# Edge segments prepared one group sooner, the last tile's chain moved ahead of the feed-forward units, and edge pairs sorted by destination so that each column's matmuls cover a band of groups

## The chip, the cores and the metric

One Trainium2 chip, one of its cores (one program, core 0). The metric is the device time of one execution in microseconds; lower is better. A core has TensorE (PE, with its weight loads shown as PEld), VectorE (DVE), ScalarE (ACT), GpSimd (POOL) and the queue engine SyncE (SP). Every engine works through its own instructions in the order in which they were written and waits on semaphores.

## The reference

A deformable 3x3 convolution, a graph attention over tokens, and a mixture of four expert networks whose weights come from the attention. All is float32.

```python
# x: (4, 128, 32, 32); channel-normalised first
o = conv3x3(xn, offset_w) + offset_b              # 27 channels: 9 dy, 9 dx, 9 masks
sampled[k] = bilinear(xn, at base + (dy, dx)[k]) * sigmoid(mask[k])       # k = 0..8, 4 corners each
x = x + einsum(sampled, dcn_w)                     # 4096 tokens of 128 channels
h = (norm(x) @ W_gat).reshape(M, HEADS, NUM_EXPERTS)
src = concatenate([edge_index[0], loops]); dst = concatenate([edge_index[1], loops])
e = leaky_relu(a_src[src] + a_dst[dst], 0.2)
ee = exp(e - max over edges into dst)
alpha = ee / segment_sum(ee, dst)
agg = segment_sum(h[src] * alpha, dst)
scores = layernorm(agg).mean(heads); top 2 of 4 experts, softmax over the two
out = x + sum over experts of gate * (gelu(norm(x) @ W1[e] + b1[e]) @ W2[e] + b2[e])
```

There are 524,288 edges with random ends in 0..32767, and M = 4096 tokens. An edge whose destination is 4096 or more is dropped, and a source of 4095 or more is read as row 4095. So an edge with a destination below 4096 either has a source below 4095 (here called a pair; about 64 in each of the 128 partitions) or it counts for the last token, and those only need a histogram of destinations.

## The kernel before

**Set-up.** Four images (b = 0..3) come in, are transposed and normalised, written to DRAM as cells (a 2 KB cell holds four corners), and convolved for the offsets. `sampling(b)` (L1009) on VectorE turns an image's offsets into gather indices `idx_i` and corner weights; it ends with a copy that raises `sampled` (L1054). All four `sampling` calls come before the loop.

**The loop over 96 groups.** 32 tiles of 128 tokens, three groups of three taps each: m = 3t + g. GpSimd issues three indirect DMAs (L455) for a group, into one of two tile buffers, and waits for `turned` of the same group two tiles earlier. ScalarE scales seven of the twelve corners (L841), VectorE the other five in one instruction (`corners`, L1076). TensorE adds the corners while transposing (`turn`, L571, 12 instructions), ScalarE evicts (L849), TensorE multiplies by the taps (`weigh`, L582), and VectorE adds the residual once per tile (`residual`, L1082).

Within the same loop, six groups (j = m % 6) to an edge segment `it` of 256 edges per partition, 16 segments: `edge_keys` makes keys that put pairs first, `keep` is one round of MAX8 and MATCH_REPLACE8 (L1158, L1160; eight rounds find the largest 56), `unpack_kept`, two one-hot instructions `hot(0)`, `hot(1)` (L1174, bf16, 128x3584), 28 histogram matmuls on TensorE (`count_edges`, L600, in the groups j = 0 and 1 of the next segment) and `add_counts` (L1128). The largest 16 keys of each segment go to `pairs1`. SyncE loads the segments into a ring of four, the first after all `sampling` calls.

From group 36 on, a unit of the feed-forward network (tile of 512 tokens, expert e; 32 units in all) is spread over every three groups: `up` twice (L625), gelu on ScalarE (L855), `down` (L636, 16 instructions) and `outputs` on VectorE (L1118). Units 0 to 19 lie in the loop.

**Between the loop and the pairs.** VectorE picks the 104 largest of the 256 keys of `pairs1` in rounds of eight (`pick_pairs`, L1218, L1219), the first 24 at once. Then follow the last residual, the last normalisation, the projection of image 3 (`project`, L615) and `token_rows` (L1137), whose rows go to DRAM (L366, L367) before GpSimd may gather source rows (L473, 10 DMAs a step). In TensorE's order units 20 and 21 stand ahead of the last tokens' transposes (L607), and units 22 and 23 ahead of `project`; units 24 to 28 follow. `unpack(0, 56)` splits the picked keys into codes; keys left over beyond 56 are collected over four partitions (`rest`), picked again (12 rounds) and spread back as 24 more columns. Low digits of the destinations are written to DRAM and broadcast to all partitions (L377), so that `turned_digits` (L1338) can build a one-hot that gathers the destination's terms with matmuls (`dst_logits`, L711).

**The pair loop.** Eight steps of ten columns, one pair per partition and column. For a column VectorE builds `code_hot` (L1311, 256 wide) and `spread` (L1312: the values times a one-hot over 16 groups of 20 values, 320 wide), and TensorE adds them into two banks (`add_pairs`, L721: four matmul instructions of 320 columns). A ring of five buffers lies between them (`NR`). In step p the next step is prepared between the columns: `hots` (L1291), `turned_digits`, then `dst_logits(p + 1)` on TensorE behind half of the columns, three multiply-and-reduce steps on VectorE (L1328, L1331), the logits, an exponential on ScalarE (L894), `weighted` (L1304). Units 29 to 31 are done in steps 0 to 3.

**The end.** Own and last-token terms (L1403 to L1412), the sums, layernorm, gates, and the gated sum of the experts (L1524), transposed and written out. If any capacity was exceeded (`lost`), a general path goes over all edges instead.

## Time and profile before

| | us |
|---|---|
| median of 3 runs | 779.71 (774.39 to 783.75) |
| the profiled execution | 772.18 |
| its span, first to last instruction | 770.4 |
| TensorE busy | 581.6 (75%) |
| VectorE busy | 549.9 (71%) |
| ScalarE busy | 363.0 (47%) |
| GpSimd busy | 411.8 (53%) |
| mean granted TensorE clock | 0.871 |
| bytes moved by DMA | 94.97 MB |

Busy shares are means over stages with different limits. A DMA issued by GpSimd occupies it for the duration shown, and another 0.30 us passes between two of them, which the profile calls "issue". "Remote" or "another core or an unknown queue" as a releaser means that the event that ended the wait was not matched to an instruction. The durations of vector instructions overlap the next one's start a little.

### The profile page before, as it was taken

The page shows a single profiled execution, that of the slowest core. Times are in us where ns is not written, and L with a number is a line of the kernel's source. Part 1 is how long each engine was busy: PE and PEld are TensorE (multiplying, and loading weights), DVE is VectorE, ACT ScalarE, POOL GpSimd, SP SyncE. Part 2 cuts the span into 40 slices and gives each one's busy share as a digit, 9 for nine tenths or more (in the row PEclk, how much of TensorE's full clock was granted, in tenths as well). Part 3 has the DMA queues.
Part 4 walks back from the last instruction along what each step waited for, and adds up shares of the span by engine and source line. Part 5 has one row for each costly group of instructions (what it writes and reads, how often), then busy time and mean ns, then how long its engine had stood idle before and what let it go on. Part 6 is the DMA issues. An engine that isn't in the chain of part 4 may idle for free.

```text
span 770.4 us, 11025 instructions
## 1 busy us (share of the span) xinstructions
PE 581.6 (75%) x3723; PEld 471.9 (61%) x3723; DVE 549.9 (71%) x1595; ACT 363.0 (47%) x1012; POOL 411.8 (53%) x401
## 2 busy tenths in 40 slices
PE   6772667756855987978978897998566799969716
PEld 4652667645754875867867695886354567646515
DVE  6825887658667583978658793794648677767897
ACT  5634456634834775856746774674312120000027
POOL 2071477667766766766876775700643455741023
PEclk9985789768878898989989997999978899979959
DMA  8661666556656666556666555600203611100002
GB/s 251 182 192 54 178 181 193 177 173 205 176 168 202 169 169 192 173 168 191 182 177 181 177 153 176 161 11 1 48 9 3 42 24 41 27 5 4 1 1 109
DMA packets 58197, 94.97 MB, mean 123 GB/s; under 512 B 21916, under 2 KB 36892, under 8 KB 58140
## 3 DMA queue, kind: packets, MB, share of 16 engines
q0 software_dynamic: 25600, 76.50, 35.1%
q1 hardware_dynamic: 32540, 17.75, 9.3%
q8 instruction: 30, 0.49, 0.3%
q14 instruction: 27, 0.22, 0.1%
HBM read 87.49 MB, written 6.71 MB: 122 GB/s over the span
## 4 chain that ended last, share of the span: by engine, by line
PE 55%; DVE 15%; issue 12%; ACT 10%; another core or an unknown queue 6%; DMA 1%; DVEq 0%; SPq 0%; ACTq 0%
PE bank L571 15%; PE bank L721 11%; PE bank L582 7%; PE bank L625 6%; ACT arena L841 5%; PE bank L636 5%; PE bank L600 4%; DVE x_tok L1524 2%; PE bank L550 2%; DVE scratch L1328 1%; PE bank L711 1%; DVE padded L1331 1%; ACT scratch L849 1%; ACT scratch L855 1%
## 5 line engine op out<-in xcount | busy, mean ns | idle before, releaser
L455 POOL DMA_INDIRECT arena<-cells,idx_i x288 | 314.1, 1090 | 179.8 <-issue 78.1
L841 ACT ACTIVATE arena<-arena,corner_w 128x128 f32<-128x128 f32 x672 | 206.5, 393 | 0.0
L571 PE MATMUL bank<-ident,arena 128*128 128x128 f32 x1152 | 168.3, 297 | 36.2 <-issue 21.2
L571 PEld LDWEIGHTS bank<-ident,arena 128*128 128x128 f32 x1152 | 146.3, 155 | 70.7 <-issue 58.2
L849 ACT COPY scratch<-bank 128x384 f32<-128x384 f32 x96 | 45.3, 472 | 164.2 <-remote 124.0
L473 POOL DMA_INDIRECT padded<-src_rows,pk_src x80 | 82.4, 1030 | 74.6 <-DVE act_gate L1345 48.1
L721 PE MATMUL bank<-scratch,arena 128*128 128x320 f32 x320 | 99.5, 465 | 23.0 <-DVE scratch L1312 21.8
L721 PEld LDWEIGHTS bank<-scratch,arena 128*128 128x128 f32 x320 | 63.6, 204 | 57.0 <-DVE scratch L1312 27.1
L582 PE MATMUL bank<-dcnw_sb,scratch 128*128 128x128 f32 x576 | 89.8, 292 | 10.9 <-issue 10.8
L582 PEld LDWEIGHTS bank<-dcnw_sb,scratch 128*128 128x128 f32 x576 | 79.4, 207 | 14.1 <-issue 14.1
L600 PE MATMUL bank<-padded 128*128 128x128 bf16 x448 | 44.2, 235 | 47.6 <-issue 47.4
L1076 DVE TENSOR_TENSOR arena<-arena,corner_w 128x640 f32<-128x640 f32 x96 | 78.8, 820 | 1.4
L636 PE MATMUL bank<-w_sb,scratch 128*128 128x128 f32 x512 | 66.1, 285 | 15.7 <-issue 13.9
L636 PEld LDWEIGHTS bank<-w_sb,scratch 128*128 128x128 f32 x512 | 63.4, 201 | 21.0 <-issue 18.5
L625 PE MATMUL bank<-chan,w_sb 128*128 128x512 f32 x128 | 70.8, 645 | 4.0 <-ACT scratch L855 2.7
L855 ACT ACTIVATE scratch<-bank,b_sb 128x512 f32<-128x512 f32 x64 | 44.0, 690 | 52.4 <-PE bank L625 21.9
L600 PEld LDWEIGHTS bank<-padded 128*128 128x128 bf16 x448 | 32.4, 105 | 56.0 <-issue 55.2
L1174 DVE TENSOR_TENSOR padded<-lanes,kept_lohi 128x3584 bf16<-128x3584 bf16 x32 | 64.6, 2019 | 0.3
L1082 DVE TENSOR_TENSOR x_tok<-bank,x_tok 128x128 f32<-128x128 f32 x32 | 9.2, 289 | 73.9 <-remote 47.3
L1158 DVE MAX8 kept<-keys 128x8 f32<-128x256 f32 x128 | 54.5, 426 | 3.2
L894 ACT ACTIVATE padded<-padded 128x40 f32<-128x40 f32 x8 | 1.9, 236 | 103.1 <-DVE padded L1300 88.2
L1160 DVE MATCH_REPLACE8 keys<-kept,keys 128x256 f32<-128x256 f32 x112 | 45.8, 408 | 0.0
(248 smaller groups left out, 661.9 us busy)
## 6 DMA issues: line engine op xcount, KB each, us to landing
arena<-cells,idx_i POOLq DMA_INDIRECT x288
scratch<-in_L_ffn_edge_index_dram SPq DMA_DIRECT2D x32, 128.0 KB
padded<-lo_rows SPq DMA_DIRECT2D x8, 320.0 KB
chan<-in_x_dram SPq DMA_DIRECT2D x4, 512.0 KB, 5.3
cells<-n_tok SPq DMA_DIRECT2D x4, 512.0 KB, 4.3
out_dram<-chan SPq DMA_DIRECT2D x8, 256.0 KB, 2.0
cells<-n_tok SPq DMA_DIRECT2D x4, 448.0 KB, 4.7
padded<-src_rows,pk_src POOLq DMA_INDIRECT x80
```

The source lines that it names most:

```text
L455: nc.gpsimd.indirect_dma_start(cell[:, u, k, :, :].rearrange("p c f -> p (c f)"), None, squares[t // TB], bass.IndirectOffsetOnAxis(ap=idx ...
L473: nc.gpsimd.indirect_dma_start(src_got[:, u, c, :], None, src_rows[:, :], bass.IndirectOffsetOnAxis(ap=pk_src[:, j:j + 1], axis=0)).then_i ...
L571: mm = nc.tensor.matmul(banks[m % 2][:, j * P:(j + 1) * P], cell[:, t % 2, 3 * g + j, c, :], ident[:, :], is_transpose=True, start=(c == 0 ...
L582: mm = nc.tensor.matmul(banks[2 + t % 2][:, 0:C], samp[:, t % 2, k, :], dcnw_sb[:, k, :], start=(k == 0), stop=(k == K - 1))
L600: mm = nc.tensor.matmul(hist, both[0], both[1], start=(c == 0), stop=(c == CAP // 2 - 1))
L625: nc.tensor.matmul(banks[4 + f][:, :], w1_sb[:, e, f * P:(f + 1) * P], chan[:, s * 512:(s + 1) * 512], start=True, stop=True).then_inc(up_ ...
L636: mm = nc.tensor.matmul(banks[6][:, q * C:(q + 1) * C], hid[:, (n % 2) * NF + f, q * P:(q + 1) * P], w2_sb[:, e, f, :], start=(f == 0), st ...
L721: mm = nc.tensor.matmul(sum_part[q], code_hot[:, r, q * P:(q + 1) * P], spread[:, r, :, :], start=False, stop=(last and col == SUB - 1))
L841: ins = nc.scalar.activation(cell[:, u, k, c, :], cell[:, u, k, c, :], ACT.Copy, scale=corner_w[:, t, k, c:c + 1])
L1076: V.tensor_tensor(spots, spots, weights.unsqueeze(2).to_broadcast([P, CORNERS - BY_ACT, C]), ALU.mult)\
L1158: done(V.max(top, ka))
L1174: ins = V.tensor_tensor(onehots[:, h, :, :].rearrange("p c (j f) -> p c j f", f=4), lanes[:, :, :].unsqueeze(1).to_broadcast([P, CAP, LO / ...
```

## The change

Twelve edits, in the order of the program:

- `sampling(2)` comes after the first segment's keys and rounds, `sampling(3)` after the first `corners`; the tiles of `sampling` lie in `arena`, and the edge loads no longer wait for it. `trow` is cleared before `sampling(0)`.
- In the loop the key rounds of segment it + 1 run in groups 3 to 5 of segment it, the one-hots in groups 1 and 2, the histogram matmuls in groups 3 and 4, `add_counts` in group 0 of the next segment.
- In the last segment's groups 3 to 5, where no next segment follows, the 56 own pairs are picked.
- Feed-forward units begin at group 33, so unit 20's `up` and `down(19)` also lie in the loop.
- The keys are turned (`turn_keys`), so that the picked pairs come sorted by destination, largest first.
- After the loop TensorE's order is `down(20)`, the digits' transpose, `up(21)`, the last tokens, `project`; units 22 to 24 follow, units 25 to 31 are done in the pair loop, one a step.
- `window(c)` gives each block of five columns a band of the 16 groups; `spread`, the matmuls on it, the one-hots and the destination terms cover the band only. A pair outside its band sets `lost`.
- The ring of `code_hot` and `spread` has 10 buffers for 5; source rows have three buffers for two; `lo_turned` has two for one.
- `dst_logits(p + 1)` comes first in TensorE's step p, and waits for `pair_lg` of the step before.
- The second and third digit broadcasts are issued earlier on SyncE.
- The own terms are worked out in steps 1 and 6 of the pair loop.
- Rounds are redistributed: 56 in the loop, 16 before `token_rows`, 32 after the first digits; the rest in 40 and 56.

```diff
-        NR = 5
+        NR = 10
...
-        PAIR_UNIT = 29
-        FIRST_UP = 36
-        HIST_SLOTS = {0: (0, 14), 1: (14, CAP // 2)}
+        PAIR_UNIT = 25
+        FIRST_UP = 33
+        HIST_SLOTS = {3: (0, 14), 4: (14, CAP // 2)}
+        BLOCK = 5
+
+        def window(c):
+
+            c0 = c // BLOCK * BLOCK
+            bounds = []
+            for k, z in ((c0 + BLOCK, 4.5), (c0 + 1, -4.5)):
+                rank = k * (1.0 - 1.0 / (9.0 * k) + z / (3.0 * k ** 0.5)) ** 3
+                bounds.append(min(max(int((1.0 - rank / 64.0) * GROUPS), 0), GROUPS - 1))
+            return bounds[0], bounds[1] + 1
...
-                        mm = nc.tensor.matmul(sum_part[q], code_hot[:, r, q * P:(q + 1) * P], spread[:, r, :, :],
-                                              start=False, stop=(last and col == SUB - 1))
+                        mm = nc.tensor.matmul(sum_part[q][:, lo * VAL:hi * VAL], code_hot[:, r, q * P:(q + 1) * P],
+                                              spread[:, r, 0:hi - lo, :], start=False, stop=(last and col == SUB - 1))
...
-            count_edges(NSEG - 1, 0, CAP // 2)
-            unit(n0)
-            unit(n0 + 1)
+            down(n0)
+            pe.wait_ge(pair_idx_ready, 1)
+            pe.wait_ge(conv_read, NT - 1)
+            early = OWN // SUB * SUB
+            nc.tensor.transpose(banks[2][0:early, 0:P], pk_lo_f[:, 0:early], ident[:, :]).then_inc(digits_turned, 1)
+            up(n0 + 1, 0)
+            up(n0 + 1, 1)
             pe.wait_ge(t_normed, B)
             turn_tokens(B - 1, 0, 0)
             pe.wait_ge(t_normed_a, 1)
             turn_tokens(B - 1, 1, 1)
-            unit(n0 + 2)
-            unit(n0 + 3)
-            pe.wait_ge(conv_read, NT - 1)
-            project(B - 1, 2)
+            pe.wait_ge(conv_read, NT)
+            project(B - 1, 3)
...
             for p in range(NSUB):
                 n = PAIR_UNIT + p
+                if p < NSUB - 1:
+                    dst_logits(p + 1)
+                if n < UNITS:
+                    up(n, 0)
+                    up(n, 1)
                 for e in range(NE):
-                    if e == NF and p < NSUB - 1:
-                        dst_logits(p + 1)
-                    if e < NF and n < UNITS:
-                        up(n, e)
-                    if e == NF and n <= UNITS:
-                        down(n - 1)
+                    if e == 3 and n < UNITS:
+                        down(n)
                     add_pairs(p, p % 2, e, last=(p == NSUB - 1))
...
+            sampling(0)
+            sampling(1)
+            edge_keys(0)
+            for rnd in range(CAP // 8):
+                keep(rnd)
+            sampling(2)
+            for m in range(3 * NT):
+                it, j = divmod(m, 6)
+                b = it // 4 - 1
+                corners(m)
+                if m == 0:
+                    sampling(3)
+                if j == 0:
+                    keep(CAP // 8)
+                    unpack_kept(it)
+                    if it >= 1:
+                        add_counts(it - 1)
+                if j == 1:
+                    done(V.tensor_copy(kept_lohi[:, :, :, :], kept_i[:, 1:3, :].unsqueeze(3).to_broadcast([P, 2, CAP, 4])))
+                    hot(0)
+                if j == 2:
+                    if it > 0:
+                        residual(2 * it - 1)
+                    hot(1)
...
+                if it + 1 < NSEG:
+                    if j == 3:
+                        edge_keys(it + 1)
+                        keep(0)
+                        keep(1)
...
+            for p in range(NSUB):
+                u = p % 2
+                spreads(p, u, 0)
+                if p < NSUB - 1:
+                    hots(p + 1, 1 - u)
+                    dst_sums(p + 1, 1 - u)
+                spreads(p, u, 1)
+                if p < NSUB - 1:
+                    logits(p + 1, 1 - u)
+                if PAIR_UNIT + p <= UNITS:
+                    outputs(PAIR_UNIT + p - 1)
+                spreads(p, u, 2)
+                if p < NSUB - 1:
+                    weighted(p + 1, 1 - u)
+                if p < NSUB - 2:
+                    turned_digits(p + 2)
+                spreads(p, u, 3)
```

## Rows read from the trace of the kernel before

**Rows 1.** Windows by stage: length; busy PE, PEld, DVE, ACT, POOL; clock, DMA share, GB/s.

```profile
78.00:294.00 216.00, 157.71 (x1158) 138.97 (x1159) 160.60 (x396) 127.35 (x397) 151.89 (x140) 0.82 0.63 183
294.00:511.00 217.00, 186.25 (x1397) 156.36 (x1397) 157.54 (x400) 139.51 (x408) 144.74 (x131) 0.91 0.58 167
511.00:588.00 77.00, 52.29 (x319) 40.44 (x317) 48.09 (x164) 25.58 (x40) 19.97 (x21) 0.90 0.08 15
588.00:730.00 142.00, 124.92 (x534) 88.81 (x534) 105.66 (x295) 13.54 (x20) 63.12 (x61) 0.92 0.20 20
```

**Rows 2.** The cell gathers of line 455: duration ns, and what ended their idle time.

```profile
L455 POOL DMA_INDIRECT arena<-cells,idx_i x288: 942/949/2725, 38.1 to 498.4; - x144
...
  remote: 35.2, 20
  PE bank L571: 33.9, 11
```

**Rows 3.** Timeline near 183 to 195 us: start, us, engine, line, operation [idle before].

```profile
184.70 0.27 PE L600 MATMUL bank<-padded 128*128 128x128 bf16 x2 [1.09 <-issue]
...
194.76 0.48 ACT L849 COPY scratch<-bank 128x384 f32<-128x384 f32 x1 [11.80 <-remote]
195.00 0.95 POOL L455 DMA_INDIRECT arena<-cells,idx_i  x1 [1.86 <-remote]
```

**Rows 4.** Timeline of VectorE: first corners of segments 4, 5, 8 and 9.

```profile
176.44 0.82 DVE L1076 TENSOR_TENSOR arena<-arena,corner_w 128x640 f32<-128x640 f32 x1
...
203.96 0.82 DVE L1076 TENSOR_TENSOR arena<-arena,corner_w 128x640 f32<-128x640 f32 x1
...
287.57 0.82 DVE L1076 TENSOR_TENSOR arena<-arena,corner_w 128x640 f32<-128x640 f32 x1
...
321.01 0.82 DVE L1076 TENSOR_TENSOR arena<-arena,corner_w 128x640 f32<-128x640 f32 x1
```

**Rows 5.** Timeline of the loop's start.

```profile
71.62 0.15 DVE L1054 COPY act_gate<-ident 128x1 f32<-128x1 f32 x1
...
78.02 0.76 DVE L1076 TENSOR_TENSOR arena<-arena,corner_w 128x640 f32<-128x640 f32 x1
...
81.99 0.95 POOL L455 DMA_INDIRECT arena<-cells,idx_i  x1 [21.26 <-PE bank L571]
```

**Rows 6.** Timeline from the last corners to the first values of the pairs.

```profile
510.79 0.82 DVE L1076 TENSOR_TENSOR arena<-arena,corner_w 128x640 f32<-128x640 f32 x1
...
515.61 0.43 DVE L1218 MAX8 pairs<-pairs 128x8 f32<-128x256 f32 x1
...
516.60 0.43 DVE L1218 MAX8 pairs<-pairs 128x8 f32<-128x256 f32 x1
...
533.29 1.88 PE L625 MATMUL bank<-chan,w_sb 128*128 128x512 f32 x4
...
535.01 1.95 PE L636 MATMUL bank<-w_sb,scratch 128*128 128x128 f32 x16
...
536.80 1.86 PE L615 MATMUL bank<-wgat_sb,chan 128*128 128x24 f32 x16
...
558.17 3.75 PE L636 MATMUL bank<-w_sb,scratch 128*128 128x128 f32 x16 [6.97 <-issue]
...
587.72 0.15 DVE L1345 COPY act_gate<-ident 128x1 f32<-128x1 f32 x1
```

**Rows 7.** Groups by shape in the pair loop (588 to 731 us): busy us, mean ns, idle.

```profile
L721 PE MATMUL bank<-scratch,arena 128*128 128x320 f32 x320 | 99.5, 465 | 23.0 <-DVE scratch L1312 21.8 <-issue 1.0
...
L1312 DVE TENSOR_TENSOR scratch<-scratch 128x320 f32<-128x320 f32 x80 | 38.7, 484 | 0.0
...
L711 PE MATMUL bank<-a_dst_heads,chan 128*128 128x128 f32 x140 | 16.9, 276 | 0.1
...
L1328 DVE TENSOR_TENSOR scratch<-bank,scratch 128x512 f32<-128x512 f32 x14 | 9.7, 692 | 24.3 <-PE bank L711 13.5 <-remote 7.6 <-issue 3.1
...
L1291 DVE TENSOR_TENSOR scratch<-iota_f,pk_group 128x160 f32<-128x160 f32 x7 | 2.2, 318 | 0.0
...
L1328 DVE TENSOR_TENSOR scratch<-bank,scratch 128x256 f32<-128x256 f32 x7 | 3.0, 424 | 0.2
```

**Rows 8.** The chain of waits, its last stretch of line 721: start, us, what.

```profile
715.37 14.28 PE bank L721 x52
```

453 lines of the change are left out of this document (239 added, 214 removed).

## The prediction

> **What bounds the kernel now.** I read the windows by stage first, then who held up GpSimd's gathers, then timelines where stages meet, then the groups of the pair loop by shape. Four stretches matter.
>
> *The loop, 78 to 511 us.* No compute engine is full: TensorE 73% and 86%, VectorE 74% and 73% of the two halves [rows 1]. GpSimd is: it shows 151.89 us for 140 gathers, and each has 0.30 us behind it, so 151.9 + 42 = 194 of 216 us, and 144.7 + 39 = 184 of 217 [rows 1]. The fastest gather takes 0.94 us, so a group of three can't take less than 3.75 us; 90 groups are 338 us of the 417 from 82.0 to 499. Of the other 79, some 39 us are gathers that take up to 2.7 us instead of 0.95 (296.6 us for 271 of them), and the rest are waits: 35.2 us "remote" and 33.9 us for line 571, of which 21.3 us is the one before the loop, so 48 us with the 0.30 us that each wait swallows [rows 2, 5]. A wait of GpSimd follows a slow stretch of TensorE like the one in rows 3: for some 10 us each pair of instructions starts 0.7 us after the last though it waits for nothing that the profile names, and ScalarE does not see the turned group for 11.80 us. GpSimd loses only 1.9 us, since it is up to six groups ahead. I count one such stretch in nearly every segment.
>
> *Loop to pairs, 511 to 588 us.* VectorE is busy 48.1 of 77 us and TensorE 52.3 [rows 1], and neither runs through: the last corners are at 510.79, the projection ends at 536.80 + 1.86 = 538.7, the first values of the pairs are there at 587.72 [rows 6]. TensorE loses 6.97 us at 558 in front of unit 26's `down`, and as much once more at 571 [rows 6].
>
> *The pair loop, 588 to 730 us.* Line 721 takes 277 ns an instruction at full clock (14.28 / 52 = 0.275) [rows 8] and has 320 of them. TensorE's work at full clock is 320 x 0.2775 = 88.8 us of columns, 140 instructions of line 711 at about 0.12 = 16.8, three pairs of ups at 1.88 and four downs at 1.95 [rows 6] = 13.4: 119 us. Actual: 142. TensorE is first, VectorE (105.7 us) not far behind, and 23 us go in handing over: TensorE waits 21.8 us for `spread`, VectorE 24.3 us for line 711 [rows 7], and part of the stretch runs at the lower clock, 0.92 in the mean [rows 1].
>
> *The end*, 770.4 - 729.7 = 40.7 us, is not touched.
>
> **The change, part by part.**
>
> *Start of the loop.* `sampling(2)` ends at 71.62, corners start at 78.02 because `sampling(3)` and the clearing of `trow` lie between [rows 5]. The first corners can follow at 71.7, so the first group is turned 6.3 us sooner and GpSimd resumes at 75.7 instead of 81.99. The second corners now wait for `sampling(3)` (78.0), the last round and the unpacking, about 79.2, against 82.2 before, and GpSimd waits some 3 us for them. From the fourth group on it is about 4.8 us ahead; I take -4.8 (ends: -3, -6.3). The first segment's keys and rounds (8 us) fall where VectorE waited 11 us for TensorE's offsets. If that cover were gone, they would delay `sampling(2)` by 8 us. The edge loads go onto SyncE's queue behind the cells' writes, with nothing behind them for a long time.
>
> *Inside the loop.* The same instructions are issued; only their groups change. VectorE's work of a segment stays some 20 us in 27, so GpSimd remains the bound and the long gathers stay. New waits: `add_counts` in group 0 waits for matmuls of two groups before (formerly of three groups before), and behind it in VectorE's order stands the next corners. `hot_ready` is already implied by the corners that TensorE waits for. A slow stretch of TensorE then holds VectorE one group's work more, about 3 us, which GpSimd's lead of six groups (22 us) still covers, as it covers 11.8 us now [rows 3]. One more unit goes in (4 us of TensorE, off the path). I take 0 for the loop. Ends: all 48 us of GpSimd's waits vanish, but one wait a segment belongs to TensorE's stretches, so a gain of 25; or every segment loses 1 us, 15.
>
> The skill has a view on those stretches. The Trainium skill, "Runtime: NRT & Kernel Launch", section on instruction fetch mechanics, says that instructions come in 16 KiB blocks of 256, fetched ahead, and that crossing a block is mostly hidden. If that were all, a TensorE that waits for nothing would not slow down, and the trace disagrees: 11.80 us behind one stretch. By it the loop would fall to GpSimd's 375 us and the total by up to 48 us more. What causes the stretches no row tells; I let them stay.
>
> *Loop to pairs.* VectorE's 48 us lose: seven rounds at 0.99 us [rows 6], moved into the last segment, -6.9; five `outputs` at 0.69, -3.4; the own logits, about -1.9; `hot(1)` and the hit mask, -3; half of the destination reductions, -1.7; one more `turned_digits` +0.9 and the bound checks +1: 33 us. Its idle 29 us shrink, because TensorE's order loses units 22 and 23 ahead of `project` (two times 1.75 + 1.75 = 7.0 us between starts [rows 6]) and the histogram, and because fewer of VectorE's steps wait for a unit: the two stretches of 7 us hit `outputs` before, and now only units 21 to 23 are consumed here. What stays late: the rows' way to DRAM and back, the digits' broadcast, and the rest's way over four partitions. They are DMA round trips, three times some 4 to 7 us, and only partly under rounds. I take 21 of the 29 us: 33 + 21 = 54 instead of 77, -23. Ends: idle 13 (46) and 29 (62). Two SyncE broadcasts moved forward stand in front of the rest's spreading, but wait on `turned_digits`, which is done by then.
>
> *Pair loop, TensorE.* The formula gives bands of 6, 8, 10, 12, 13, 14, 14, 13, 12, 11, 10, 9, 9, 8, 7 and 6 groups of 20 values for the sixteen blocks of five columns: 162 of 256, 63%. A 24-column instruction takes 1.86 / 16 = 0.116 us [rows 6]; that is the floor. Above it I scale 0.2775 by columns / 320 (0.104 for six groups, hence 0.116; 0.243 for fourteen). The sixteen blocks sum to 2.83 us, times 20 instructions: 56.6 us instead of 88.8, -32. Line 711 is already near the floor (0.12 at 128 columns), so its narrowing gives nothing. Units 25 to 31 cost 7 x (1.88 + 1.95) = 26.8 instead of 13.4. Total 56.6 + 16.8 + 26.8 = 100 us instead of 119.
>
> *Pair loop, VectorE.* From 484 ns at 320 and 318 at 160 elements, an element costs 1.04 ns [rows 7]; 202 on average instead of 320 saves 0.12 us a column, 9.8 in all. The reductions (692 at 512, 424 at 256: 1.05 ns) narrow by 30%: -5.6; the one-hots -1. Four more `outputs` +2.8, own logits +1.9. So 105.7 - 16.4 + 4.7 = 94 us. The two engines are nearly even, 100 and 94, and taken step by step the larger of the two (TensorE in steps 2 and 3 with 16 us, VectorE in the first two and step 6 with 13 to 15) sums to 108.
>
> *Handing over.* The ring of 10 and the early `dst_logits` remove what made TensorE wait 21.8 us, yet nearly even engines wait for one another more, and at step 2 and 3 VectorE must wait for TensorE's last three columns. Of the 23 us that 142 has above 119 I let 9 stay above 108: 117, so -25. Ends: 108 (nothing left) and 128 (the same 19% on top). The third buffer of source rows lets GpSimd run further ahead, off the path.
>
> **Sum.** 770.4 - 4.8 + 0 - 23 - 25 = 717.6 us of span, about 719 for the profiled execution (before: 772.2). The median of the runs lies 7.5 us above the profiled execution. With the same distance: 727 us.
>
> **Rivals.**
> - *The hand-over keeps the gain* (0.2). Shorter matmuls only make TensorE wait for VectorE, whose 94 us plus the waits for line 711 become the bound: pair loop 128 (+11); and the two 7 us stretches stay on the path ahead of it (+8), with one more in the denser pair loop (+4). 750 us. For it: both engines are near 100 us. Against: the ring is twice as deep.
> - *The loop gains too* (0.12). The histogram moved behind the groups that need it lets GpSimd's waits shrink by 25 to 30 us: 700 us. For it: 48 us of such waits. Against: the stretches are not caused by VectorE.
> - *The loop gets slower* (0.05), the other side. Segment 4 takes 27.5 us, segment 8 takes 33.4, and there the slow stretch fell on turns and weighs and VectorE waited for a conv result, and not on the histogram [rows 4]. If moving the histogram puts the stretch on the turns in every segment, each of 15 costs 5.9 us more: +88, 815 us. It decides from 53 / 15 = 3.5 us a segment.
> - *The change doesn't do what it says* (0.01). One pair outside its band starts the general path, thousands of gathers at 1.25 us: milliseconds. The bands are cut at 4.5 deviations, so I give it almost nothing.
>
> **How the numbers follow.** The forecast has 0.62, with its own ends 712 (unprofiled, pair loop 108, idle 13) and 742. The range takes in the first rival and part of the second: 706 to 754. Faster by over 1% (about what can be told from no change) holds for the first three cases: 0.94; slower takes the last two, 0.05; within 1%: 0.01.
>
> **What would show it.** Right: the first gather after the pause near 76 us; the last corners near 506; the projection's end 18 to 19 us after them and not 28; the pair loop's start some 54 us after them; line 721 in shapes from 120 to 280 columns with 57 to 65 us at full clock; the pair loop at 110 to 125 us; the last 41 us as before. Wrong: segments of 30 us and more, which means the loop; TensorE idle behind `spread` for over 20 us in the pair loop; or gaps of 7 us called "issue" between the projection and the pairs.

## The result, and the profile after

The kernel after takes 770.55 us in the median of 20 runs, the kernel before 777.9 us on the same chip; the ratio is 0.9875, with a 95% interval of 0.984 to 0.991. Ratios, here and below, leave out executions more than 1.5% longer than the fastest of the same kernel, while the medians include them. So it is 1.2% faster, where the forecast said 727 us, 6.5% faster, and 706 to 754. The profiled execution took 774.0 us and its span is 772.3.

The stages, cut at events that every kernel has (all from the timelines; "band matmuls" are those of `add_pairs`, L721 before and L753 after; the forecast's column is its own sum):

| us from the span's start | before | forecast | after |
|---|---|---|---|
| first corners | 78.0 | about 71.7 | 74.7 |
| GpSimd resumes | 82.0 | 75.7 | 78.7 |
| last corners | 510.8 | 506 | 514.2 |
| first values of the pairs | 587.7 | 560 | 595.1 |
| first band matmul | 588.6 | 561 | 601.1 |
| last band matmul ends | 729.6 | 677 | 731.5 |
| span | 770.4 | 717.6 | 772.3 |

Against the forecast the last corners come 8 us late, the way to the pairs' first values takes 81 us instead of 54 (+27), the pair loop 136.4 instead of 117 (+19), and the end is as forecast. In spans the miss is 54.7 us and in medians 43.5, because the 7.5 us that the forecast added from three runs of the kernel before did not come again: here the median lies 3.5 us below the profiled execution. Before's lines for the same stretches are in [rows 1]. After, by windows (an engine's busy us and instructions, then granted clock, DMA share, GB/s):

```profile
core 0: us, PE busy (x) PEld busy (x) DVE busy (x) ACT busy (x) POOL busy (x), PEclk, DMA share, GB/s
...
514.00:595.00 81.00, 43.57 (x246) 35.67 (x245) 37.12 (x143) 17.25 (x33) 29.57 (x31) 0.73 0.10 19
595.00:731.50 136.50, 109.99 (x600) 93.44 (x599) 92.83 (x312) 28.94 (x36) 49.37 (x51) 0.87 0.19 18
731.50:772.30 40.80, 14.76 (x97) 12.89 (x96) 33.32 (x97) 21.80 (x62) 10.72 (x16) 0.75 0.14 52
```

Work did go. VectorE does 37.1 us between the loop and the pairs (48.1 before; the forecast left it 33, so 4 us of what it took off stayed) and 92.8 in the pair loop (105.7; forecast 94). TensorE's band matmuls lost what was forecast, 31.5 us of busy time against 32 (all forms, 320 instructions, busy us and mean ns; before 99.5 and 465 in the same view):

```profile
L753 PE MATMUL bank<-scratch,arena 128*128 128x120 f32 (+8 forms) x320 | 68.0, 363 | 26.2 <-DVE scratch L1286 14.1 <-issue 12.1
```

Yet the time stayed. The largest piece of the chain of waits says where, 25.4 us in one piece, and the waits name three engines at the same moment:

```profile
558.64 25.40 another core or an unknown queue
```

```profile
584.11 1.26 ACT L895 ACTIVATE scratch<-bank,b_sb 128x512 f32<-128x512 f32 x2 [37.21 <-remote]
584.13 0.69 DVE L1152 TENSOR_TENSOR arena<-bank,b_sb 128x512 f32<-128x512 f32 x1 [25.49 <-remote]
...
585.42 1.43 PE L665 MATMUL bank<-w_sb,scratch 128*128 128x128 f32 x5 [25.09 <-ACT scratch L895]
```

VectorE stood for 25.5 us in front of an `outputs` (L1152) whose matmuls (L665) had ended at 558.3; ScalarE stood in front of matmuls (L654) that had ended at 560.3, and TensorE behind ScalarE. Only one engine worked, GpSimd. The windows over that stretch:

```profile
550.00:558.00 8.00, 7.72 (x36) 7.75 (x37) 4.70 (x17) 0.00 (x0) 6.06 (x7) 0.50 0.25 54
558.00:566.00 8.00, 2.34 (x6) 0.81 (x5) 0.61 (x3) 0.00 (x0) 5.98 (x7) 0.93 0.10 9
566.00:575.00 9.00, 0.00 (x0) 0.00 (x0) 0.00 (x0) 0.00 (x0) 6.87 (x8) 0.50 0.11 11
575.00:584.00 9.00, 0.00 (x0) 0.00 (x0) 0.00 (x0) 0.00 (x0) 3.19 (x4) 0.50 0.05 5
```

GpSimd issues the gathers of the pairs' source rows, and these move little: 10% of the DMA engines, some 10 GB/s. Nothing else was under way: the digits' broadcast that SyncE had issued at 552.85 shows in the 54 GB/s of 550 to 558 us and no longer in the 9 to 11 GB/s behind it. With the third buffer it issued 30 in one unbroken row (0.30 us between two of them), where before it issued 20 (544.0 to 569.3) and then waited for `pair_used`:

```profile
541.10 1.19 POOL L501 DMA_INDIRECT padded<-src_rows,pk_src  x1 [3.85 <-DMA dst_rows<-a_dst]
542.58 0.94 POOL L501 DMA_INDIRECT padded<-src_rows,pk_src  x1 [0.30 <-issue]
...
578.17 0.94 POOL L501 DMA_INDIRECT padded<-src_rows,pk_src  x1 [0.30 <-issue]
...
595.56 1.00 POOL L501 DMA_INDIRECT padded<-src_rows,pk_src  x1 [16.45 <-DVE act_gate L1330]
```

VectorE's last instruction ends at 558.7 us and TensorE's at 560.3, 18 to 19 us and 14 to 15 gathers after the row began, and they resume at 584.1, 5 us after its last gather ended. A second row of 20, from 595.6 to 620.9, has a slow stretch at 607 to 624 us. This one sets in 11 us and 9 gathers after its row began, and from 609.6 us on a broadcast of SyncE is under way in it (DMA share 0.85 in 607 to 616 us, at 9 GB/s). In the trace of before the row of 20 ends at 569.3, and the VectorE step that the prediction's "second stretch of 7 us" hit starts at 569.8. The edge loop has rows of up to 18 gathers, and the slow stretch of [rows 3] lies at the end of one of them (below).

### The profile page after: what moved, and what is told of

It is laid out like the page before. It is cut to its first block, busy times and chain, and to the rows that moved or that the text cites. A ratio compares the mean times of both kernels' runs of the same rounds, so it can differ in the third digit from the quotient of the medians.

```text
span 772.3 us, 11071 instructions
## 1 busy us (share of the span) xinstructions
PE 563.0 (73%) x3723; PEld 475.0 (62%) x3723; DVE 534.5 (69%) x1609; ACT 370.6 (48%) x1018; POOL 407.7 (53%) x433
## 4 chain that ended last, share of the span: by engine, by line
PE 49%; DVE 18%; issue 12%; another core or an unknown queue 10%; ACT 9%; DMA 2%; SPq 0%; DVEq 0%; ACTq 0%
PE bank L598 13%; PE bank L609 6%; PE bank L753 6%; PE bank L654 6%; ACT arena L881 5%; PE bank L665 5%; PE bank L578 4%; PE bank L629 3%; DVE x_tok L1604 2%; PE bank L742 2%; DVE arena L1110 1%; DVE padded L1209 1%; PE bank L644 1%; ACT scratch L889 1%
## 5 line engine op out<-in xcount | busy, mean ns | idle before, releaser
L598 PE MATMUL bank<-ident,arena 128*128 128x128 f32 x1152 | 166.4, 294 | 39.4 <-issue 22.4
L598 PEld LDWEIGHTS bank<-ident,arena 128*128 128x128 f32 x1152 | 144.6, 153 | 77.3 <-issue 62.4
L889 ACT COPY scratch<-bank 128x384 f32<-128x384 f32 x96 | 45.3, 472 | 166.0 <-remote 125.3
L501 POOL DMA_INDIRECT padded<-src_rows,pk_src x80 | 78.2, 978 | 72.0 <-DVE act_gate L1330 45.3
L609 PE MATMUL bank<-dcnw_sb,scratch 128*128 128x128 f32 x576 | 91.5, 293 | 14.6 <-issue 13.2
L753 PE MATMUL bank<-scratch,arena 128*128 128x120 f32 (+8 forms) x320 | 68.0, 363 | 26.2 <-DVE scratch L1286 14.1
L665 PE MATMUL bank<-w_sb,scratch 128*128 128x128 f32 x512 | 66.8, 286 | 25.5 <-ACT scratch L895 25.3
L665 PEld LDWEIGHTS bank<-w_sb,scratch 128*128 128x128 f32 x512 | 64.0, 202 | 27.5 <-ACT scratch L895 26.2
L753 PEld LDWEIGHTS bank<-scratch,arena 128*128 128x128 f32 x320 | 56.6, 204 | 37.8 <-issue 16.7
L654 PE MATMUL bank<-chan,w_sb 128*128 128x512 f32 x128 | 73.3, 667 | 3.6 <-issue 3.6
L629 PE MATMUL bank<-padded 128*128 128x128 bf16 x448 | 41.3, 237 | 35.2 <-issue 34.9
L1116 DVE TENSOR_TENSOR x_tok<-bank,x_tok 128x128 f32<-128x128 f32 x32 | 9.3, 289 | 71.2 <-remote 52.8
L1152 DVE TENSOR_TENSOR arena<-bank,b_sb 128x512 f32<-128x512 f32 x24 | 16.5, 686 | 29.1 <-remote 25.5
```

The lines of the kernel that those rows point to most:

```text
L501: nc.gpsimd.indirect_dma_start(src_got[:, u, c, :], None, src_rows[:, :], bass.IndirectOffsetOnAxis(ap=pk_src[:, j:j + 1], axis=0)).then_i ...
L598: mm = nc.tensor.matmul(banks[m % 2][:, j * P:(j + 1) * P], cell[:, t % 2, 3 * g + j, c, :], ident[:, :], is_transpose=True, start=(c == 0 ...
L609: mm = nc.tensor.matmul(banks[2 + t % 2][:, 0:C], samp[:, t % 2, k, :], dcnw_sb[:, k, :], start=(k == 0), stop=(k == K - 1))
L629: mm = nc.tensor.matmul(hist, both[0], both[1], start=(c == 0), stop=(c == CAP // 2 - 1))
L654: nc.tensor.matmul(banks[4 + f][:, :], w1_sb[:, e, f * P:(f + 1) * P], chan[:, s * 512:(s + 1) * 512], start=True, stop=True).then_inc(up_ ...
L665: mm = nc.tensor.matmul(banks[6][:, q * C:(q + 1) * C], hid[:, (n % 2) * NF + f, q * P:(q + 1) * P], w2_sb[:, e, f, :], start=(f == 0), st ...
```

## The experiments

**Theory A:** a long unbroken row of GpSimd's indirect gathers makes the other engines' issue and the events between them late, from some 16 to 18 us after its start until GpSimd pauses; the third buffer made the row longer and so gave back what the rest of the change gained. **Theory B:** the stretches are TensorE's own (its instruction supply), and the missing time has other causes: the third buffer's traffic, the denser pair loop, VectorE as the bound. Each group of runs had its own runs of the kernel before on its chip: 770.45 us in the median for the first four, 771.21 for the next four, 777.91 for the four after those, 775.21 for the last three. A ratio is to those.

**One step less of lead in the pair loop** (the kernel after; a lead of two steps, three buffers)

```
-                if p >= GOT:
-                    pool.wait_ge(pair_used, p - GOT + 1)
+                if p >= 2:
+                    pool.wait_ge(pair_used, p - 1)
```

> The changed kernel with GpSimd allowed two pair steps ahead instead of three (the third source buffer stays). Theory A (an uninterrupted run of GpSimd's gathers holds back TensorE's issue and its semaphores until GpSimd pauses): GpSimd stops after 20 gathers, at about 566 us, so the stretch that began near 558 and ended at 584.1 ends near 570; the pairs start some 12 to 14 us sooner and the time is 755 to 760 us, ratio to the kernel before 0.97 to 0.975. Rival B (the stretch has nothing to do with the third buffer, but with what TensorE or the digit broadcasts do): the stretch stays about 25 us long, time 768 to 773, ratio 0.985 to 0.99.

738.78 us, ratio 0.958 [0.954, 0.962]: a larger gain than either theory expected. The first row of gathers is 20 long again (526.7 to 552.0), and the `outputs` behind it waits 10.75 us, until 555.26, instead of 25.49. From the last corners to the first band matmul it is 71.2 us instead of 86.9. One wait in GpSimd's order is worth 3% of the kernel.

The profiled executions are 34 us apart, and 14 of these lie ahead of the edit: the last corners come at 500.4 us instead of 514.2. That stretch has the same instructions in both. In the other variants whose order is untouched up to there (full width; paced pairs twice, and at full width; the iotas between pair steps) they come between 504.6 and 511.2 us. So the place of a stage in a single execution can be off by 5 to 10 us, and the profiled execution of the kernel after is the slowest of these there.

**The third buffer alone, in the kernel before** (`src_got` with three buffers, GpSimd up to three steps ahead)

> The kernel before with three buffers of source rows instead of two, nothing else. Theory A: GpSimd's run in front of the pairs grows from 20 to 30 gathers (544 to about 581 us), the wait of 5.75 us that VectorE had at 569.8 grows by up to 12 us, time +8 to +12 us, ratio 1.01 to 1.015. Rival B: the same time, ratio 1.0 within 0.3%, or slightly faster since GpSimd is further ahead.

780.46 us (768.8 to 783.6; 4 runs) beside 770.45 (758.1 to 779.8): +10 us in the median, but the runs overlap and no interval is on record. Its first row is 30 long (548.5 to 586.2) and from the last corners to the first band matmul it takes 92.6 us instead of 77.8. Part of the 15 us comes back in its pair loop, 129.3 instead of 141.0 us. The stages bear out theory A, the longer row and the later pairs; that this part of the change is a loss in time by itself is likely and not shown.

**Windows of the full width** (the kernel after)

```
-            return bounds[0], bounds[1] + 1
+            return 0, GROUPS
```

> The changed kernel with every band set to all 16 groups, so each column's matmuls have 320 columns again and VectorE builds 320 elements. If the sum of the prediction holds, TensorE's work in the pair loop rises from 100 to 132 us at full clock and the time by 20 to 32 us, to 790 to 802, ratio 1.015 to 1.03. Rival: the pair loop is bound by handing over and by slow stretches and not by the columns, so the narrowing is worth 10 us or less: 771 to 781, ratio 0.99 to 1.004.

768.02 us in the median, ratio 1.004 [0.998, 1.010]. Against the kernel after nothing is lost by the medians, but these were taken beside runs of before that differ by 7 us (770.45 and 777.9). The ratios, each to its own runs of before, lie 1.6% apart (0.9875 there) and their intervals do not meet: some 12 us, between the two expectations. The band matmuls take 89.4 us instead of 68.0, and from the first to the last of them it is 137.6 us instead of 130.4. The row of 30 is there, and the 25.0 us wait too.

**Four groups of lead in the edge loop instead of six** (the kernel after)

```
-                        pool.wait_ge(turned, 3 * (t - 2) + g + 1)
+                        pool.wait_ge(turned, 3 * (t - 2) + g + 3)
```

> The changed kernel with the cell gathers of the loop held to four groups ahead of the turned group instead of six (waits for two more groups to be turned). Theory A: the slow stretches of TensorE last until GpSimd pauses; with a shorter lead GpSimd pauses sooner, so they shrink from some 10 us to 3 us and the waits of ScalarE (11.8 us) with them; the loop keeps its length or gets up to 20 us shorter: 750 to 771 us. Rival B: the stretches have a length of their own (10 us); a lead of four groups (15 us) less the landing no longer covers them, and the loop grows by 3 to 6 us a stretch, 16 of them: 815 to 865 us.

755.71 us, ratio 0.976 [0.971, 0.982]. ScalarE's "remote" waits for the turned groups fall from 125.3 us (the longest 11.8) to 65.2 (4.9). The row of 30 and its 25.0 us wait stay. In the profiled executions the edge loop takes 432.6 us instead of 439.5 and the stretch of the band matmuls 124.8 instead of 130.4.

**Pairs paced** (the kernel after, the lead of three steps kept; GpSimd waits between two steps until the ten gathers of the earlier one have landed)

```
                 if p >= GOT:
                     pool.wait_ge(pair_used, p - GOT + 1)
+                if p >= 1:
+                    pool.wait_ge(pair_in[(p - 1) % 3], 16 * SUB * ((p - 1) // 3 + 1))
```

> The kernel after, with GpSimd held in the pair loop until the ten gathers of its previous step have landed; its lead of three steps stays. Theory A (a run of more than some 14 gathers without a pause of GpSimd makes the other engines' issue and their semaphores late until it pauses; the kernel after starts 30 in a row at the loop's end): the run of 30 falls apart into three of ten, so the 25 us remote waits near 559 to 584 us go or shrink below 8 us, the pairs start some 60 us after the last corners instead of 81, the pair loop has no stretch of 1.0 to 1.7 us issue pieces, and the time is 725 to 742 us, as with a lead of two steps (738.8) or below it. Theory B (the lead of three steps itself costs, by the DMA traffic of the rows or by their buffers): the lead is the same as in the kernel after, so 765 to 775 us.

726.23 us, ratio 0.932 [0.925, 0.939]; 44 us less than the kernel after in the medians, 43 by the ratios, and that by one wait. The rows of ten have pauses of 3.4, 1.7 and 2.1 us between them (536.3 to 549.2, 552.6 to 564.8, 566.5 to 578.7, 580.8 to 594.0):

```profile
548.27 0.94 POOL L503 DMA_INDIRECT padded<-src_rows,pk_src  x1 [0.30 <-issue]
552.61 0.94 POOL L503 DMA_INDIRECT padded<-src_rows,pk_src  x1 [3.40 <-DMA padded<-src_rows,pk_src]
...
566.47 0.97 POOL L503 DMA_INDIRECT padded<-src_rows,pk_src  x1 [1.69 <-DMA padded<-src_rows,pk_src]
```

Its stages, from the last corners on:

```profile
509.60:571.90 62.30, 48.68 (x267) 39.15 (x266) 40.60 (x153) 18.17 (x32) 24.16 (x26) 0.78 0.14 29
571.90:693.00 121.10, 105.13 (x577) 89.07 (x575) 90.09 (x301) 28.15 (x35) 56.98 (x57) 0.92 0.22 17
693.00:734.00 41.00, 14.54 (x96) 12.71 (x96) 33.50 (x97) 21.80 (x62) 10.38 (x16) 0.75 0.14 52
```

62.3 us to the first band matmul instead of 86.9, with the same instructions, and no standstill on that way; then 121.1 instead of 130.4. In the pair loop a slow stretch stayed, in a row of ten that began at 580.8, behind a pause of 2.1 us:

```profile
584.00:597.00 13.00, 8.23 (x33) 6.86 (x33) 2.06 (x8) 0.00 (x0) 7.88 (x8) 0.63 1.10 14
```

```profile
596.64 0.66 DVE L1313 TENSOR_TENSOR arena<-bank,scratch 128x480 f32<-128x480 f32 x1 [10.94 <-remote]
```

VectorE waited 10.9 us there, and the DMA share was 1.10 while 14 GB/s moved, with a broadcast of SyncE under way. So the pauses removed the standstill of 25 us and not every slow stretch. Theory B about the lead falls: lead and buffers are those of the kernel after. So does B about the instruction supply for the standstill, since TensorE's and VectorE's programs are unchanged.

**The edge loop paced as well** (at every fourth group GpSimd waits for the landing of the group before)

```
+                    m = 3 * t + g
+                    if m >= 4 and m % 4 == 0:
+                        tp, gp = divmod(m - 1, 3)
+                        pool.wait_ge(cells_in[3 * (tp % 2) + gp], 48 * (tp // 2 + 1))
```

> The kernel after with the pairs paced as in the run before, and in the loop too: at every fourth group GpSimd waits until the gathers of the group before it have landed, so no run is longer than 12 gathers. Theory A: TensorE's slow stretches in the segments (0.7 us between pairs of instructions for some 10 us) vanish, the waits of line 571 and of the turns' groups with them; each pause costs some 2 us of GpSimd, 24 of them 48 us, against 47.5 us of GpSimd's waits that the loop has now, so the loop (424 us) comes out between 385 and 425 us and the whole at 690 to 740 us. Theory B (the stretches come from TensorE's own instruction supply): the stretches stay, the pauses are added, and the loop grows by 20 to 48 us over the run with paced pairs.

762.72 us, ratio 0.990 [0.985, 0.995], 36 us slower than with paced pairs alone. The late events mostly went, and GpSimd's own pauses cost more than they gave:

```profile
POOL arena L487 <- DMA arena<-cells,idx_i: 77.2, 21, 5.8
...
ACT scratch L895 <- remote: 55.7, 17, 8.6
...
DVE x_tok L1122 <- remote: 15.0, 6, 5.3
```

Line 895 is here what line 889 is in the kernel after. There ScalarE's waits were 125.3 us and VectorE's 52.8. But 77.2 us of pauses replace 41.0 us of GpSimd's "remote" waits, and from the first to the last corners it is 476 us instead of 438. The first corners came at 65.6 us instead of 71.7: the row of 18 gathers ahead of the loop is cut too.

**Both paced, windows of the full width**

> As the run before (both paced), but with windows of the full width. It asks what the narrow bands are worth once no stretch lies over the pair loop. The prediction's reasoning (columns bind TensorE in the pair loop: 32 us of columns less) makes it 15 to 30 us slower than the run before; the reasoning that VectorE and the hand-over bind makes it slower by 0 to 8 us, as full width was worth nothing measurable with the long runs in place.

776.94 us, ratio 0.997 [0.990, 1.004]: 14 us slower than the run before by the medians, 0.7% by the ratios. The stretch of the band matmuls is 136.7 us instead of 113.2 in the profiled executions; but this one's was the longest of its ten runs (788 us), so the two stretches can't be set side by side; the intervals of the two ratios overlap.

**The kernel before with both pacings**

> The kernel before with both pacings (its two buffers of source rows kept). Theory A: it gains too, since its loop has runs of 18 gathers and its pairs runs of 20: the two stretches of TensorE near 558 and 571 us shrink to one or none (-7), the stretch at 660 to 677 us goes (-5 to -10), the loop changes as it does in the run with both paced. So 730 to 765 us. The distance to the kernel after with both paced is then the change's own worth without the run of 30, and the prediction said 43 to 50 us. Theory B: 770 to 800 us, as only the pauses are added.

780.03 us, ratio 1.005 [0.999, 1.011]. It missed. Its pair loop has 129.7 us instead of 141.0, but the way to it stays (76.5 us), and its edge loop grew to 463.7 from 432.8.

**The kernel before with paced pairs alone**

> The kernel before, with only the pair loop's gathers paced to runs of ten (its two buffers of source rows kept, its other loop untouched). Before has a first run of 20. Both pacings cost its edge loop some 30 us and left its pair loop at 129.7 us of line 721 instead of 141, and the way from the last corners to it at 76.5 instead of 77.8. If the runs of 20 cost before only inside its pair loop: 758 to 764 us. The distance from there to the kernel after with paced pairs (726.2) is the change's own worth, 32 to 38 us. If pacing is worth as much to before as to after (44 us), it would come to 727 to 735 us, and the change would be worth nothing; if nothing, 771.

769.23 us, ratio 0.987 [0.982, 0.991] (0.9866 of 777.9), by the ratio in the expected place. So pacing is worth 1.3% to before and 5 to 5.5% to after. The way to the pairs takes 79.1 us and the band stretch 140.8 us, both unchanged, and no stage of the profiled execution (775.66 us) shows where the 1.3% lies. VectorE's wait in front of `outputs` stayed as well, 5.45 us until 578.22 where it was 5.75. The pause between its first two rows of ten was 1.6 us, against 3.4 in the kernel after. Either it was too short or that wait has another cause; no run tells.

**Pairs paced, windows of the full width** (the kernel after)

> The kernel after with paced pairs (726.2 us), and windows of the full width. With long runs in place full width cost nothing measurable; with both loops paced it cost 14 us in the medians. If TensorE's columns bind the pair loop once no stretch lies over it: 738 to 750 us, the matmuls of line 753 taking 30 us more and the stretch from the first to the last of them 130 to 140 us instead of 121. If VectorE and the hand-over bind it: 726 to 732 us.

736.61 us, ratio 0.943 [0.937, 0.949], against 0.932 and 0.936 (below) with narrow windows: narrow bands are worth 0.7 to 1.1%, 5 to 9 us, though the intervals overlap. The band matmuls take 92.0 us instead of 65.2 (26.8), and the stretch 134.8 instead of 121.1 and 117.4 us; this profiled execution was the longest of its four (750.92 us), so the stretch is rather too long. The pair loop with full width, beside the row of 121.10 us above, shows where the rest goes:

```profile
core 0: us, PE busy (x) PEld busy (x) DVE busy (x) ACT busy (x) POOL busy (x), PEclk, DMA share, GB/s
...
573.60:708.40 134.80, 126.63 (x577) 91.29 (x575) 105.58 (x302) 29.48 (x37) 56.67 (x56) 0.99 0.19 16
```

At full width TensorE is busy 94% of the stretch and keeps a clock of 0.99, narrow it is busy 87% at 0.92. The 26.8 us of columns came back as 21.5 us of busy time, at least in part because narrow it does part of its work at the lower clock (1.2 instead of 2.4 GHz; 0.63 was granted from 584 to 597 us), and of those 21.5 another 8 went into standing (16.0 us instead of 8.2).

**Paced pairs and four groups of lead**

> The kernel after with paced pairs and with a lead of four groups instead of six in the edge loop (alone worth 1.5 to 2.5% of 770). If the two add: 726.2 - 10 to 15 = 711 to 717 us, the edge loop 430 to 434 us. If both bought the same (the shorter run in front of the pairs), 724 to 730 us.

741.02 us, ratio 0.953 [0.949, 0.957]: slower than paced pairs alone, so the two don't add. Its edge loop took 439.1 us from first to last corners, with a lead of six it took between 433.1 and 439.5 in the kernel after and its variants. With the row of 30 in place the same edit had gained 1.1% (0.976 against 0.9875), here it loses 1.7 to 2%; why is not known. A shorter lead is no gain that can be relied on.

**Two iotas between the steps instead of a wait**

```
+                if p >= 1:
+                    for h in range(2):
+                        ...
+                        nc.gpsimd.iota(fill_i[:, h, :], [[1, 288]], base=0, channel_multiplier=0)
```

> The kernel after, where GpSimd makes two iotas of 128x288 (1.0 us each, into a tile that nothing reads) between one step's ten gathers of the pair loop and the next; no wait for anything to land. It asks what ends a stretch: a pause in the stream of gathers, or the landing of what is under way. If a pause of the stream of 2 us is enough: as with paced pairs, 722 to 735 us, the way from the last corners to the first matmul of line 753 about 62 us instead of 87. If the gathers under way must land: the stretch stays, 765 to 775 us.

756.89 us, ratio 0.970 [0.963, 0.976]: neither. The iotas took 0.70 us together, not 2, so from the third step on the stream paused for 0.9 us only. Ahead of the first two, GpSimd stood 6.94 us that the profile calls "issue", so the first pause was 7.8 us long (548.2 to 556.0):

```profile
555.14 0.69 POOL L505 IOTA fill_i<- 128x288 int32 x2 [6.94 <-issue]
```

The way to the pairs is free (62.1 us), but behind that long pause it says nothing about pauses of 0.9 us. These are tested in the pair loop: 40 gathers with them between the tens run from 556.0 to 608.2, and TensorE is slow from 588 to 612.6. Here one sees what a slow stretch looks like:

```profile
589.43 0.37 PE L672 MATMUL bank<-w_sb,scratch 128*128 128x128 f32 x1 [1.53 <-issue]
...
592.26 0.37 PE L672 MATMUL bank<-w_sb,scratch 128*128 128x128 f32 x1 [1.53 <-issue]
592.26 0.18 DVE L1263 TENSOR_TENSOR pk_out<-pk_out 128x24 f32<-128x24 f32 x1 [4.00 <-remote]
...
592.98 0.18 DVE L1264 SCALAR_TENSOR_TENSOR pk_out<-pk_void,pk_out 128x24 f32<-128x24 f32 x1 [0.53 <-DVE pk_out L1263]
593.66 0.18 DVE L1266 TENSOR_REDUCE lost_out<-pk_out 128x1 f32<-128x24 f32 x1 [0.51 <-DVE pk_out L1264]
594.35 0.37 PE L672 MATMUL bank<-w_sb,scratch 128*128 128x128 f32 x1 [1.72 <-issue]
595.07 0.16 DVE L1267 TENSOR_TENSOR lost<-lost,lost_out 128x1 f32<-128x1 f32 x1 [1.22 <-DVE lost_out L1266]
```

The starts of both engines lie on one grid of 0.70 us, mostly one of the two at a time and at 592.26 both. That points to something that they share; what it is, no run shows. The prediction's slow stretch has the same 0.7 us [rows 3].

**Eight iotas between the steps**

> The kernel after with eight iotas of 128x288 between one step's ten gathers of the pair loop and the next. Two of them took 0.70 us together and put only 0.9 us between the runs: the slow stretch then came later (some 30 us after the stream had resumed) but held from 588 to 612 us. Eight make a pause of 2.8 us or more, about the 1.7 to 3.4 us that the wait for landing made with paced pairs, and wait for no gather. If a pause of the stream of that length is what ends a stretch: no stretch between the last corners and the end of the pair loop, 0.932 to 0.945 of the time of the kernel before. If the gathers must have landed: 0.965 to 0.985.

735.01 us, ratio 0.947 [0.941, 0.954]. Eight iotas put 2.8 us between two rows, and 9.9 us between the first two, where GpSimd stood 7.12 us as in the run before; the way to the pairs is 60.7 us and no standstill lies on it:

```profile
566.17 2.62 POOL L505 IOTA fill_i<- 128x288 int32 x8
568.95 1.00 POOL L508 DMA_INDIRECT padded<-src_rows,pk_src  x1 [0.16 <-issue]
```

The ratio lies just past the range for "a pause is enough" and far from "they must have landed". So pauses of the stream bring most of it, without a wait for landing. They do not bring all: the band stretch is 127.3 us, 6 to 10 more than with the wait, and two standstills of over 7 us lie in it, in rows of ten with 2.8 us between them. The first ends as its row ends (597.4):

```profile
597.35 0.20 DVE L1277 TENSOR_TENSOR padded<-padded 128x40 f32<-128x40 f32 x1 [7.71 <-issue]
...
615.28 0.63 DVE L1318 TENSOR_TENSOR arena<-bank,scratch 128x448 f32<-128x448 f32 x1 [7.60 <-remote]
```

**Six iotas at every fourth group of the edge loop** (pairs paced)

> The kernel after with paced pairs, and in the edge loop six iotas (2.1 us or a little more) ahead of every fourth group instead of a wait for landing (which took 3.3 us and made the edge loop 38 us longer, 476 instead of 438 us, while its slow stretches went). If pauses of 2.1 us also end the stretches: ScalarE's remote waits for the turned groups fall from 127 to some 60 us as they did with the waits for landing, GpSimd loses 23 x 2.1 = 48 us and gets back the 41 us of its own remote waits and some 15 of line 600's: the edge loop 425 to 450 us, the time 0.925 to 0.95 of before. If they don't end them: the loop some 45 us longer, 0.98 to 0.99.

741.07 us in the median, but with a spread of 733 to 751. ScalarE's waits for the turned groups fell to 109.6 us, not to 60, and from the first to the last corners it takes 449.7 us. The first expectation asked for both, 425 to 450 us and 60 us of waits; the loop is at its end and the waits are not. Against the paced pairs alone (437.9 and 433.1 us) nothing was gained in the edge loop, though only 12 to 17 of the 48 us of pauses show in its length.

**Paced pairs once more**

> The kernel after with paced pairs, once more, so that the others of this group have it on the same chip: 0.925 to 0.94 of before.

729.01 us, ratio 0.936 [0.926, 0.946]; its way to the pairs takes 62.7 us, its band stretch 117.4.

## Why the prediction was wrong

The kernel after with paced pairs ran at 726.2 and 729.0 us in the median; the forecast was 727. That agreement is luck. The forecast's sum is a span, 717.6 us, and the spans of the two profiled executions with paced pairs are 734.0 and 726.3; and pacing also breaks up rows of 20 that the kernel before had and that the forecast left as they were. These two executions have the instructions of the kernel after on TensorE, VectorE and ScalarE, and each term is set beside them:

| us, profiled executions | before | forecast | after | lead of two steps | pairs paced (two runs) |
|---|---|---|---|---|---|
| first corners | 78.0 | 71.7 | 74.7 | 67.4 | 71.7, 72.4 |
| first to last corners | 432.8 | about 434 | 439.5 | 433.1 | 437.9, 433.1 |
| last corners to first values of the pairs | 76.9 | 54 | 80.9 | 65.8 | 55.5, 56.1 |
| from there to the last band matmul | 141.9 | 117 | 136.4 | 131.2 | 127.9, 124.0 |
| the end | 40.8 | 40.7 | 40.8 | 40.6 | 41.0, 40.7 |

- *"The third buffer of source rows lets GpSimd run further ahead, off the path."* This step failed. GpSimd is off the path, but its gathers are not harmless to the engines on it. With the buffer the row went from 20 to 30, and VectorE's wait behind it from 5.75 us to 25.49. Taking back the lead alone gives 3% (ratio 0.958 instead of 0.9875, 23 us), about half of the 43.5 us that the result missed. With the rows cut to ten it is 40 to 43 us by the ratios and 44 in the medians (770.5 to 726.2); in the profiled executions 34 and 37 us of it lie behind the last corners. So the other half is no correction of this step: it is a gain that the forecast did not count, and it covers what its pair loop promised too much.
- *Pair loop and handing over, -25.* This term was mis-sized. With paced pairs the stretch is 14 and 18 us shorter than before, with a lead of two steps 11, in the kernel after 5.5. TensorE's columns lost what was forecast (31.5 us against 32), but that is worth less in time: full width costs 5 to 12 us. VectorE's work was right (92.8 us in the kernel after, 93.5 and 94.1 paced, against 94). The 9 us left for handing over were too few, and 6 of the stretch are new: with `dst_logits` and `up` first in TensorE's step, the first band matmul starts 6.0 us after the first values (595.1 to 601.1), before 0.9. How much of the gain comes from the deeper ring, the early terms of the next step and the pauses, these runs don't part.
- *Loop to pairs, -23.* -21 with paced pairs (55.5 and 56.1 us against 54), where the long row is gone. The parts were less exact: VectorE is busy 37.2 us in both, not 33, and idle for 18 and 19, not 21. In the kernel after the standstill took all of it back.
- *Start of the loop, -4.8.* First corners at 74.7 in the kernel after, 71.7 and 72.4 paced (before 78.0), against 71.7 worked out. The size is right, the place is less fixed than the prediction took it: variants of the kernel after whose start is the same lie between 67.4 and 74.8 us, and the three with a pause within the first 18 gathers at 60.4, 64.6 and 65.6. That row ahead of the loop seems to cost some 7 us too.
- *Inside the loop, 0.* From first to last corners before took 432.8 us, variants of before 435.2 and 435.6, after and its variants with an untouched loop 433.1 to 439.5. Right: 0 to +7, and the kernel after's own execution is at the upper end. The rival in which segments grow by 5.9 us is out.
- *The end, 0.* 40.8 us in both.

The change's own worth with both kernels paced is 0.9866 against 0.9321 and 0.9361: 5 to 5.5%, 39 to 43 us, where the forecast's terms sum to 53.

Of the rivals, *the hand-over keeps the gain* (750 us) came nearest and had part of the place right (*"the two 7 us stretches stay on the path"*), not the price. None said that the change itself makes them longer. Of the signs in "what would show it" one came, larger than named: a gap between the projection and the pairs, of 25 us and called "remote". TensorE was idle behind `spread` for 14.1 us in the pair loop (the row of line 753), not for over 20.

The prediction took the two gaps of 6.97 us before `down` for stretches of one kind. The first is a plain wait: `down` needs the `outputs` before it, and VectorE was busy with rounds until it did that at 557.34; the gap is there in the kernel before with paced pairs too (6.74 us). Only the second follows a late event, VectorE's at 569.81.

It let the stretches stay because *"no row tells"* what causes them. Rows did: in the trace of before the slow stretch of [rows 3] ends at 194.65 us, 1.5 us after a row of GpSimd's gathers ended (193.14), and the one before `outputs` at 569.8, 0.5 us after. The prediction weighed them against the Trainium skill, "Runtime: NRT & Kernel Launch", section on instruction fetch mechanics, where crossing a block of instructions is said to be mostly hidden, and read 11.80 us [rows 3] as the trace's disagreement. With paced pairs TensorE runs the same instructions past the same place without the 25 us, so that standstill was not about fetching. The waits of the kind of [rows 3] fell from 125.3 to 55.7 us when GpSimd paused in the edge loop, with the same instructions on TensorE. So the 11.80 us are no evidence against the page.

**What stays open.** What GpSimd's gathers and the other engines share. In the standstill it isn't the DMA engines' capacity (share 0.10); in the pair loop's stretches the share is 0.85 to 1.10 at 9 to 14 GB/s, with a broadcast of SyncE under way, so these may have a second cause. What sets the onset is open too: 14 to 15 gathers into the row of 30, 9 into the row of 20 behind it, and in rows of ten a few gathers after a pause of 2 to 3 us. And why the edge loop gains nothing when its late events go: fewer late events and more pauses came out at +38 us and, with shorter pauses, at some +14.

## What to carry to other kernels

When several engines stop together and the releaser is "remote" or "issue", look at which engine is still busy, and compare the ends of the stops with the ends of its rows of instructions, before calling the stop a constant. More buffers for an engine that is ahead aren't always free: here they lengthened its unbroken row. A wait that delays nothing needed (10 gathers, then a pause of 2 to 3 us) was worth 44 us, six times the effect of the whole change as it was made, and the same wait in a loop where that engine is the bound cost more than it gave. And a forecast that agrees with a changed kernel's time is checked stage by stage: here a term that was too large and a gain that was not counted cancelled.

## What the runs showed of the hardware

- During and right behind unbroken rows of 20 to 30 indirect gathers of GpSimd (1.25 us each) the other engines run late or stand: in the kernel after from 18 us after the row's start, or from 11 us in the second row, TensorE down to an instruction in 0.7 to 2.8 us, or three engines at 0.00 us busy for 18 us, until 0.5 to 5 us after the row's end.
- Pauses of 1.7 to 3.4 us after every ten gathers removed the standstill of 25 us ahead of the pairs (ratio 0.932 instead of 0.9875). In the pair loop slow stretches stayed: 10.9 us in a run with the wait for landing, 7.7 and 7.6 us with pauses of 2.8 us, and some 24 us with pauses of 0.9 us.
- A gather's row in the profile ends well before its data are there: after the tenth, which ended at 549.21 us, GpSimd's wait for landing let the next start at 552.61, 3.4 us later. The Trainium skill, "Perfetto Trace Analysis", section on the DMA instruction of GpSimd's software path, says that the profile's end is that of making the descriptors; the trace agrees.
- Two iotas of 128x288 in one dimension took 0.70 us together among the first gathers of the pairs; the same size in a pattern of three or four dimensions took 1.01 and 0.97 us each in the set-up.
